# Softmax weights of two attention layers turned by SBUF transfers and 32x32 blocks on VectorE instead of on TensorE

## Chip, cores, metric

The kernel runs on one core of a Trainium2 chip. The metric is the device time in microseconds of one execution, taken as the median of several runs; a profile of one further execution gives the trace.

## What is computed

A stack of four graph layers works on 32 batch elements of 512 nodes with 256 channels, in float32, with one 512 x 512 adjacency for all. Each layer adds its result to its normalised input's residual:

```python
h = relu(layernorm(x)); x = x + layer(h, adj)
# layer 0: one head
e = leaky_relu((h @ W1) @ (h @ W2).T, 0.2), masked by adj
x += relu(softmax(e) @ (h @ W3))
# layers 1 and 3: four heads of 64, additive scores
e[i, j] = leaky_relu(dst[i] + src[j]), masked; x += elu(softmax(e) @ (h @ W))
# layer 2: four heads of 64, dot products
e = (Q K.T) / 8, masked
x += layernorm((softmax(e) @ V) @ Wo + bo) * gamma + beta
```

The softmax weights of layers 0 and 2 come out of the exponential with the query node on the partitions. The aggregation contracts over the other node, so they are needed with that one on the partitions: a transposition of a 512 x 512 matrix, once in layer 0 and four times (once a head) in layer 2, per batch element. Layers 1 and 3 form their weights turned from the start, since their scores are sums.

## The kernel before

A 512 x 512 matrix lies in SBUF as 128 partitions x 4 rows (t) x 512. The kernel is a software pipeline over the batch, with an order written out by hand for each engine. `slots` (L286) calls `first` for element 0, then `slot(a, b, c, d)` for n = 1 to 33 with a = element n, b = n - 1, c = n - 2, d = n - 3 (None outside 0 to 31). In one slot a goes through layer 0 and the beginning of layer 1, b through the rest of layer 1 and the beginning of layer 2, c through the rest of layer 2 and layer 3. Buffers are in three sets, s = element mod 3; the table BANK (L126) gives each product in PSUM one or two of eight banks. Semaphores alone bind the engines together, each engine runs its list strictly in order: `slot` for SP at L328, GpSimd L420, ScalarE L590, VectorE L841, TensorE L1158.

The work that the change and the steps of the prediction touch:
- `exp0` (L472) and `exp2` (L556), ScalarE, write one row t of the weights of layer 0 and of head h of layer 2, from what `masked_max0` (L662) and `masked_max2` (L781) on VectorE left.
- `weights_transposed0` (L1012) and `weights_transposed2` (L1110), TensorE: four 128 x 128 transposes of one row into a PSUM bank; `weights_out0` and `weights_out2` copy the bank to SBUF, half of them on ScalarE (L482, L565), half on VectorE (L692, L800).
- `aggregate0` (L1021) and `aggregate2` (L1129), TensorE, use the turned weights; the latter takes the heads in two pairs. `inverse_columns`, `inverse_spread` and `inverse_out` (L575 to L584, L1119) bring the inverse row sums into the layout of that product, `norm2` (L817) multiplies, `o_rows` (L1149) and `o_out` (L825) are the output product and its bias (L829 in the trace).
- `scores0`, `scores2`, `u_columns`, `v_rows`, `q_rows`, `qk_columns`, `transposed` (L958 to L1106) are the other products; `gat_weights` (L738) on VectorE and `gat_aggregate` (L1070) on TensorE are layers 1 and 3.
- `spread` (L316) on SP's queue writes the row factors of a layer of that kind to DRAM, waits, and reads them back broadcast to all partitions in two transfers; `gat_weights` waits for these. For two (element, layer) pairs, the first element's layer 1 and the last one's layer 3, TensorE broadcasts the first two heads itself (BY_PE, L218; L1066).
- `idle_turns` (L963) issues filler matmuls in the slots at either end.
- `load_next` and `store` (L312, L303), SP's queue, fetch x three elements ahead and write the result.

## Time and profile before

| | us |
|---|---|
| median of 3 runs | 2944.53 (2944.07 to 2944.73) |
| the profiled execution | 2943.7 |
| TensorE busy in it | 2887.3 (98%) |
| VectorE busy | 2127.5 (72%) |
| ScalarE busy | 1682.3 (57%) |
| GpSimd busy | 827.8 (28%) |
| HBM traffic | 105.5 MB, 36 GB/s over the span |

Busy time counts an engine's instructions, not its semaphore waits or the issuing of DMAs. Matmuls overlap each other, so TensorE's busy time is read as "never long without work" and the price of a matmul as the distance between two of them. The profiled span is 0.8 us below the median of the runs.

### The profile page before, as it was taken

What the parts mean: (1) busy time and instruction counts of PE and PEld (TensorE: products, weight loads), DVE (VectorE), ACT (ScalarE), POOL (GpSimd) and SP (SyncE); (2) the same over time, 40 slices, a digit from 0 to 9 for tenths busy, and PEclk for the clock granted to TensorE, in tenths of its full rate; (3) what the DMA queues carried; (4) which work ended last, traced back from release to release, by engine and by line L of the source; (5) the groups of instructions that cost most, each with busy time, mean ns of one, the idle gap of its engine ahead of it and who ended that gap; (6) DMA issues with size and microseconds to landing.
All of it is one profiled execution on the core that took longest, in us unless ns stands there. A gap on an engine that the chain in (4) does not pass through costs nothing.

```text
span 2943.7 us, 68275 instructions
## 1 busy us (share of the span) xinstructions
PE 2887.3 (98%) x27732; PEld 2034.8 (69%) x27732; DVE 2127.5 (72%) x5596; ACT 1682.3 (57%) x3554; POOL 827.8 (28%) x917
## 2 busy tenths in 40 slices
PE   7899999999999999999999999999999999999998
PEld 5566767666767666767667767667767667776766
DVE  5576787776787776877776877776877777877764
ACT  2555655655656655656655656656656656656543
POOL 2123222323222323222233232233222233222221
PEclk9999999999999999999999999999999999999999
DMA  3001011101011101011101011101011111011010
GB/s 102 22 23 45 27 41 45 44 23 45 23 44 45 44 23 44 23 44 44 38 30 44 23 45 44 37 30 44 23 45 44 34 33 40 28 37 37 17 36 30
DMA packets 58840, 109.89 MB, mean 37 GB/s; under 512 B 5568, under 2 KB 41408, under 8 KB 58528
## 3 DMA queue, kind: packets, MB, share of 16 engines
q1 hardware_dynamic: 58032, 104.61, 10.8%
q8 instruction: 220, 3.60, 0.5%
q0 software_dynamic: 496, 0.92, 0.3%
q14 instruction: 92, 0.75, 0.1%
HBM read 88.21 MB, written 17.30 MB: 36 GB/s over the span
## 4 chain that ended last, share of the span: by engine, by line
PE 77%; DVE 12%; POOL 6%; issue 2%; ACT 1%; SPq 0%; DMA 0%; POOLq 0%; DVEq 0%; ACTq 0%
PE ps L972 19%; PE ps L1080 11%; PE ps L1106 8%; PE ps L1115 8%; PE ps L978 8%; PE ps L1142 8%; PE ps L1029 8%; PE ps L958 4%; DVE stats L641 3%; POOL rstd L367 3%; POOL xc L417 3%; DVE pB L753 2%; PE ps L1017 2%; DVE nb L658 1%; DVE hn L829 1%
## 5 line engine op out<-in xcount | busy, mean ns | idle before, releaser
L389 POOL TENSOR_TENSOR qx<-qx,xc 128x512 f32<-128x512 f32 x128 | 163.7, 1279 | 869.4 <-ACT qx L529 869.4
L641 DVE BATCH_NORM_STATS2 stats<-xc 128x6 f32<-128x256 f32 x384 | 134.7, 413 | 328.6 <-POOL xc L399 264.1
L448 ACT ACTIVATE hn<-xc,nb,rstd 128x256 f32<-128x256 f32 x384 | 209.1, 592 | 163.9 <-DVE nb L658 160.7
L1080 PEld LDWEIGHTS ps<-vals,pA 128*64 128x64 f32 x8192 | 253.9, 138 | 54.6 <-issue 54.5
L972 PE MATMUL ps<-wgat,hT 128*128 128x264 f32 x1024 | 267.4, 395 | 1.8 <-ACT hT L457 1.8
L1080 PE MATMUL ps<-vals,pA 128*64 128x65 f32 x8192 | 266.4, 223 | 2.1 <-DVE pA L753 2.0
L1080 PE MATMUL ps<-vals,pB 128*64 128x65 f32 x8192 | 264.0, 223 | 0.3 <-DVE pB L753 0.2
L1080 PEld LDWEIGHTS ps<-vals,pB 128*64 128x64 f32 x8192 | 249.7, 138 | 16.8 <-issue 16.7
L457 ACT COPY hT<-ps 128x1024 f32<-128x1024 f32 x128 | 129.7, 1013 | 224.0 <-PE ps L958 219.8
L1106 PE MATMUL ps<-qx,qT 64*128 64x512 f32 x1024 | 249.8, 614 | 1.1 <-DVE hn L767 0.8
L364 POOL TENSOR_SCALAR rstd<-mv 128x4 f32<-128x4 f32 x160 | 75.0, 469 | 610.2 <-DVE mv L650 610.2
L1029 PE MATMUL ps<-vals,pB 128*128 128x256 f32 x1024 | 243.2, 381 | 1.1 <-ACT vals L469 1.1
L1142 PE MATMUL ps<-pX,vals 128*64 128x512 f32 x512 | 233.6, 599 | 2.3 <-DVE pA L806 2.3
L978 PE MATMUL ps<-hT,wqkvo 128*128 128x512 f32 x512 | 233.0, 598 | 0.8 <-ACT hT L457 0.8
L1008 PE MATMUL ps<-hT,qT 128*128 128x512 f32 x512 | 228.3, 599 | 1.1 <-ACT qT L463 1.1
L1029 PEld LDWEIGHTS ps<-vals,pB 128*128 128x128 f32 x1024 | 190.6, 191 | 38.9 <-issue 14.8
L972 PEld LDWEIGHTS ps<-wgat,hT 128*128 128x128 f32 x1024 | 179.5, 190 | 50.4 <-issue 24.9
L958 PE MATMUL ps<-ident,hn 128*128 128x128 f32 x1024 | 199.0, 280 | 11.9 <-ACT hn L448 11.1
L958 PEld LDWEIGHTS ps<-ident,hn 128*128 128x128 f32 x1024 | 132.3, 141 | 105.3 <-DVE rowmax L667 32.7
L367 POOL TENSOR_TENSOR rstd<-rstd,minus_half 128x4 f32<-128x4 f32 x160 | 192.5, 1203 | 13.3
L753 DVE SCALAR_TENSOR_TENSOR pA<-qT,gval,adjT 128x512 f32<-128x512 f32 x248 | 184.5, 785 | 6.7 <-DMA hT<-r_dram 6.5
L562 ACT ACTIVATE pX<-pX,negmax 128x512 f32<-128x512 f32 x256 | 183.4, 720 | 0.6 <-DVE negmax L797 0.6
(147 smaller groups left out, 6194.3 us busy)
## 6 DMA issues: line engine op xcount, KB each, us to landing
qT<-r_dram SPq DMA_DIRECT2D x64, 512.0 KB, 3.9
hT<-r_dram SPq DMA_DIRECT2D x64, 512.0 KB, 4.9
x_in<-in_x SPq DMA_DIRECT2D x32, 512.0 KB, 3.9
out_x<-xc SPq DMA_DIRECT2D x32, 512.0 KB, 3.0
...
r_dram<-growT SPq DMA_DIRECT2D x64, 8.0 KB, 1.3
...
```

The source lines that it names most:

```text
L367: nc.gpsimd.tensor_tensor(rstd[s][:, :], rstd[s][:, :], minus_half[:, :], ALU.pow).then_inc(rstd_ready[norm].sem, 1)
L641: last = nc.vector.bn_stats(stats[s][:, t, :], src[:, t, :])
L753: last = nc.vector.scalar_tensor_tensor(out=gat_p[s][h % 2][:, t, :], in0=row, scalar=gval[s][:, 1, t, h:h + 1], in1=adjT[:, t, :], op0=AL ...
L958: last = nc.tensor.transpose(ps[:, bank + k, t * P:(t + 1) * P], hn[s][:, t, k * P:(k + 1) * P], ident[:, :])
L972: last = nc.tensor.matmul(at, src[w.s][:, k, t * P:(t + 1) * P], wt[:, k, 0:width], start=(k == 0), stop=(k == KT - 1))
L978: last = nc.tensor.matmul(ps[:, bank + m, :], wt[:, k, m * P:(m + 1) * P], hT[w.s][:, k, :], start=(k == 0), stop=(k == KT - 1))
L1008: last = nc.tensor.matmul(ps[:, BANK[f"E{t}"], :], qT[s][:, k, t * P:(t + 1) * P], hT[s][:, k, :], start=(k == 0), stop=(k == KT - 1))
L1029: last = nc.tensor.matmul(rows_in(BANK["A"])[:, t, :], pB[s][:, t, j * P:(j + 1) * P], vals[s][:, j, 0:C], start=(j == 0), stop=(j == NT - 1))
L1080: last = nc.tensor.matmul(ps[lo:hi, BANK[f"G{g}.{h}"], t * DV:(t + 1) * DV], gat_p[s][h % 2][:, j, t * P + lo:t * P + hi], vals[s][:, j, h ...
L1106: last = nc.tensor.matmul(ps[:, BANK[f"S{p}.{t}"] + hh, :], qT[s][at, p, t * P:(t + 1) * P], kT[s][at, p, :], start=True, stop=True)
L1115: last = nc.tensor.transpose(ps[:, BANK[f"PT{h}.{t}"], j * P:(j + 1) * P], prob2[w.s][h][:, t, j * P:(j + 1) * P], ident[:, :])
L1142: last = nc.tensor.matmul(ps[hh * D:(hh + 1) * D, BANK[f"G2.{p}"], :], vals[s][:, j, h * D:(h + 1) * D], probT2[s][h][:, :, j * P:(j + 1) ...
```

## The change

The five transpositions per element no longer use TensorE and PSUM. SP's queue issues for each 512 x 512 tile of weights 16 SBUF to SBUF transfers: the tile is cut into 4 bands of 32 partitions, and a transfer takes from source band a the column blocks of 32 that belong to b, and writes them to band b of a scratch tile. VectorE then transposes all 32 x 32 blocks of one 128 x 512 row at a time from the scratch tile back over the weights (`turned0`, `turned2`). There are two scratch tiles; a third and later move waits until VectorE has emptied its tile. The moves come in a fixed order, layer 0 of a, then the four heads of b, each after all four exponentials of its tile.

The order lists of all engines are new, now over `slot(z, a, b, c, d, e)` with z = n + 1 for n = 1 to 34: layer 0's statistics of z are taken one slot early, the last half of layer 3's norms, its elu and its store belong to d. The PSUM table is new. x has two input buffers instead of three; some semaphores are shared. BY_PE is dropped (both pairs go through `spread`), and the filler matmuls in the ordinary slots are dropped, those of `first` stay.

```diff
+    X_SETS = 2
+    RING = 2
+    LAST = 3
...
-        x_in = sets("x_in", [P, NT, C])
+        x_in = [sb(f"x_in{s}", [P, NT, C]) for s in range(X_SETS)]
...
-        probT2 = [[pX[2], pA[s], pB[s], pX[2]] for s in range(SETS)]
+        probT2 = prob2
...
+        scratch = [pX[2], sb("scratch1", [P, NT, N])]
...
-        BY_PE = {(0, 1): (1, 3), (B - 1, 3): (1, 0)}
-        r_by_pe = sem("r_by_pe")
-
-        def lone(w, g):
-            return list(BY_PE).index((w.c, g)) if (w.c, g) in BY_PE else None
...
+        MOVES = (
+            (0, (0,)), (1, (2, 0)), (1, (2, 1)), (1, (2, 2)), (1, (2, 3)),
+        )
...
+            def emptied(self, eng, w, tile):
+                i = self.at[w.c, tile]
+                if i >= RING:
+                    c, old = self.steps[i - RING]
+                    (pT0_dve if old[0] == 0 else pT2_dve[old[1]]).wait(eng, Work(c), NT)
...
+        def bands(tile, band, column):
+
+            rows_of = tile[32 * band:32 * (band + 1), :, :].rearrange("p t n -> p (t n)")
+            return rows_of.rearrange("p (j b c) -> p j b c", b=P // 32, c=32)[:, :, column, :]
+
+        def move(sp, w, tile, weights):
+            slot = moves.slot_of(w, tile)
+            for a in range(P // 32):
+                for b in range(P // 32):
+                    sp.dma_start(bands(scratch[slot], b, a), bands(weights, a, b)).then_inc(moves.sems[slot], 16)
...
+            def move0(w):
+                if w is None:
+                    return
+                p0_ready.wait(sp, w, NT)
+                moves.emptied(sp, w, (0,))
+                move(sp, w, (0,), pA[w.s])
+
+            def move2(w, h):
+                if w is None:
+                    return
+                p2_ready[h].wait(sp, w, NT)
+                moves.emptied(sp, w, (2, h))
+                move(sp, w, (2, h), prob2[w.s][h])
+
+            def slot(z, a, b, c, d, e):
+                spread(b, 1); load_next(b); store(d); move0(a); spread(c, 3); move2(b, 0); move2(b, 1); move2(b, 2)
+                move2(b, 3)
...
-            def weights_out0(w, t):
-                if w is None:
-                    return
-                pT0p_ready.wait(act, w, t + 1)
-                nc.scalar.copy(pB[w.s][:, t, :], ps[:, BANK[f"PT{t}"], :]).then_inc(pT0_act.sem, 1)
...
+            def slot(z, a, b, c, d, e):
+                elu_relu(d, 3, 0); elu_min(d, 3, 0); elu_exp(d, 3, 0); elu_relu(d, 3, 1); elu_min(d, 3, 1)
+                elu_m[3].wait(act, d, 2); normalised(a, 0, 0); normalised(a, 0, 1); normalised(a, 0, 2)
+                normalised(a, 0, 3); elu_exp(d, 3, 1); h_transposed(a, 0); normalised(c, "in", 0)
+                normalised(c, "in", 1); normalised(c, "in", 2); normalised(c, "in", 3); u_out(a); elu_min(b, 1, 0)
+                elu_relu(b, 1, 0); elu_exp(b, 1, 0); elu_relu(b, 1, 1); elu_min(b, 1, 1); elu_exp(b, 1, 1)
+                v_out(a, 0); normalised(c, 3, 0); normalised(c, 3, 1); normalised(c, 3, 2); normalised(c, 3, 3)
+                h_transposed(c, 3); normalised(b, 2, 0); normalised(b, 2, 1); normalised(b, 2, 2); normalised(b, 2, 3)
+                h_transposed(b, 2); q_out(c, 3, 0); exp0(a, 0); exp0(a, 1); exp0(a, 2); exp0(a, 3); q_out(c, 3, 1)
+                biased_out(b, "KT", 0); biased_out(b, "QT", 0); biased_out(b, "QT", 1); gat_row_exp(c, 3)
+                biased_out(b, "KT", 1); gat_exp(c, 3); exp2(b, 0, 0); exp2(b, 0, 1); exp2(b, 0, 2); exp2(b, 0, 3)
+                exp2(b, 1, 0); exp2(b, 1, 1); exp2(b, 1, 2); relu0(a, 0); relu0(a, 1); relu0(a, 2); relu0(a, 3)
+                exp2(b, 1, 3); inverse_columns(b, 0); exp2(b, 2, 0); exp2(b, 2, 1); exp2(b, 2, 2); exp2(b, 2, 3)
+                exp2(b, 3, 0); normalised(a, 1, 0); normalised(a, 1, 1); normalised(a, 1, 2); normalised(a, 1, 3)
+                exp2(b, 3, 1); h_transposed(a, 1); inverse_out(b, 0); exp2(b, 3, 2); exp2(b, 3, 3); q_out(a, 1, 0)
+                inverse_columns(b, 1); q_out(a, 1, 1); gat_row_exp(a, 1); gat_exp(a, 1); inverse_out(b, 1)
+                v_out(b, 2)
...
+            def turned0(w, t):
+                if w is None:
+                    return
+                moves.landed(dve, w, (0,))
+                nc.vector.transpose(pA[w.s][:, t, :], scratch[moves.slot_of(w, (0,))][:, t, :]).then_inc(pT0_dve.sem, 1)
+
+            def turned2(w, h, t):
+                if w is None:
+                    return
+                moves.landed(dve, w, (2, h))
+                nc.vector.transpose(prob2[w.s][h][:, t, :],
+                                    scratch[moves.slot_of(w, (2, h))][:, t, :]).then_inc(pT2_dve[h].sem, 1)
+
+            def slot(z, a, b, c, d, e):
+                gat_norm(d, 3, 2); turned2(c, 2, 2); turned2(c, 2, 3); gat_norm(d, 3, 3); turned2(c, 3, 0)
+                turned2(c, 3, 1); turned2(c, 3, 2); turned2(c, 3, 3); norm2(c, 0); gat_out(d, 3, 0); gat_out(d, 3, 1)
+                gat_weights(b, 1, 0, 0, 1); norm2(c, 1); gat_weights(b, 1, 0, 2, 3); gat_weights(b, 1, 1, 0, 1, 2, 3)
+                o_out(c); statistics(c, "in"); mean_and_variance(c, "in"); gat_weights(b, 1, 2, 0, 1, 2, 3)
+                shift_of_norm(c, "in"); gat_weights(b, 1, 3, 0, 1, 2, 3); times_gamma(c); gat_norm(b, 1, 0)
+                gat_norm(b, 1, 1); gat_norm(b, 1, 2); gat_norm(b, 1, 3); statistics(c, 3); mean_and_variance(c, 3)
+                gat_out(b, 1, 0); mv_ready[3].wait(dve, c, 2); statistics(z, 0); gat_out(b, 1, 1); shift_of_norm(c, 3)
+                statistics(b, 2); mean_and_variance(b, 2); masked_max0(a, 0); masked_max0(a, 1); lrelu0(a, 0)
+                shift_of_norm(b, 2); lrelu0(a, 1); masked_max0(a, 2); mean_and_variance(z, 0); masked_max0(a, 3)
+                softmax_shift0(a); second_vectors(a); lrelu0(a, 2); lrelu0(a, 3); inverse_sum0(a); gat_max_t(c, 3); gat_max(c, 3)
+                gat_shift(c, 3); masked_max2(b, 0, 0, 0); masked_max2(b, 0, 0, 1); gat_rows_out(c, 3)
+                masked_max2(b, 0, 1, 0); masked_max2(b, 0, 1, 1); masked_max2(b, 0, 2, 0); masked_max2(b, 0, 2, 1)
+                turned0(a, 0); masked_max2(b, 0, 3, 0); masked_max2(b, 0, 3, 1); softmax_shift2(b, 0); turned0(a, 1)
+                masked_max2(b, 1, 0, 0); turned0(a, 2); masked_max2(b, 1, 0, 1); turned0(a, 3)
+                gat_weights(c, 3, 0, 0, 1, 2, 3); gat_weights(c, 3, 1, 0); masked_max2(b, 1, 1, 0)
+                masked_max2(b, 1, 1, 1); masked_max2(b, 1, 2, 0); masked_max2(b, 1, 2, 1); inverse_sums2(b, 0)
+                masked_max2(b, 1, 3, 0); masked_max2(b, 1, 3, 1); statistics(a, 1); softmax_shift2(b, 1)
+                mean_and_variance(a, 1); gat_weights(c, 3, 1, 1); turned2(b, 0, 0); turned2(b, 0, 1); turned2(b, 0, 2)
+                shift_of_norm(a, 1); turned2(b, 0, 3); gat_weights(c, 3, 1, 2, 3); gat_weights(c, 3, 2, 0, 1)
+                turned2(b, 1, 0); turned2(b, 1, 1); turned2(b, 1, 2); turned2(b, 1, 3); gat_norm(c, 3, 0)
+                gat_weights(c, 3, 2, 2); inverse_sums2(b, 1); gat_weights(c, 3, 2, 3); gat_weights(c, 3, 3, 0, 1)
+                shift_of_norm(z, 0); gat_max_t(a, 1); gat_weights(c, 3, 3, 2); gat_max(a, 1); turned2(b, 2, 0)
+                gat_weights(c, 3, 3, 3); gat_shift(a, 1); gat_norm(c, 3, 1); turned2(b, 2, 1); gat_rows_out(a, 1)
...
-            def weights_transposed2(w, h, t):
-                if w is None:
-                    return
-                p2_ready[h].wait(pe, w, t + 1)
-                for j in range(NT):
-                    last = nc.tensor.transpose(ps[:, BANK[f"PT{h}.{t}"], j * P:(j + 1) * P],
-                                               prob2[w.s][h][:, t, j * P:(j + 1) * P], ident[:, :])
-                last.then_inc(pT2p_ready[h].sem, 1)
...
+            def slot(z, a, b, c, d, e):
+                aggregate2(c, 0); pT2_dve[3].wait(pe, c, 4); aggregate2(c, 1); transposed(a, 0, 0)
+                transposed(a, 0, 1); transposed(a, 0, 2); transposed(a, 0, 3); o_rows(c, 0); o_rows(c, 1)
+                o_rows(c, 2); o_rows(c, 3); u_columns(a, 0); gat_aggregate(b, 1, 0); o_ready.wait(pe, c)
+                gat_aggregate(b, 1, 1); u_columns(a, 1); v_rows(a, 0, 0); gat_aggregate(b, 1, 2)
+                gat_aggregate(b, 1, 3); v_rows(a, 0, 1); gnorm[1].wait(pe, b, 3); scores0(a, 0); v_rows(a, 0, 2)
+                v_rows(a, 0, 3); scores0(a, 1); v0_ready.wait(pe, a); scores0(a, 2); transposed(c, 3, 0)
+                transposed(c, 3, 1); transposed(c, 3, 2); transposed(c, 3, 3); scores0(a, 3); masked0.wait(pe, a, 2)
+                q_rows(c, 3, 0); transposed(b, 2, 0); q_rows(c, 3, 1); transposed(b, 2, 1); transposed(b, 2, 2)
+                transposed(b, 2, 3); q_rows(c, 3, 2); q_rows(c, 3, 3); qk_columns(b, "QT", 0); masked0.wait(pe, a, 4)
+                qk_columns(b, "KT", 0); qk_columns(b, "KT", 1); qk_columns(b, "QT", 1); gat_max_across(c, 3)
+                gat_max_spread(c, 3); scores2(b, 0, 0); qT_ready.wait(pe, b, 2); scores2(b, 0, 1); gat_rows(c, 3)
+                kT_ready.wait(pe, b, 2); scores2(b, 0, 2); masked2[0].wait(pe, b, 2); scores2(b, 0, 3)
+                masked2[0].wait(pe, b, 4); scores2(b, 1, 0); scores2(b, 1, 1); pT0_dve.wait(pe, a); aggregate0(a, 0)
+                pT0_dve.wait(pe, a, 2); aggregate0(a, 1); pT0_dve.wait(pe, a, 3); aggregate0(a, 2)
+                pT0_dve.wait(pe, a, 4); aggregate0(a, 3); masked2[0].wait(pe, b, 8); scores2(b, 1, 2)
+                masked2[1].wait(pe, b, 2); scores2(b, 1, 3); agg0_norm.wait(pe, a, 4); gat_aggregate(c, 3, 0)
+                masked2[1].wait(pe, b, 6); v_rows(b, 2, 0); v_rows(b, 2, 1); v_rows(b, 2, 2); v_rows(b, 2, 3)
+                transposed(a, 1, 0); transposed(a, 1, 1); inverse_spread(b, 0); transposed(a, 1, 2)
+                transposed(a, 1, 3); gat_aggregate(c, 3, 1); q_rows(a, 1, 0); q_rows(a, 1, 1); gnorm[3].wait(pe, c)
+                q_rows(a, 1, 2); q_rows(a, 1, 3); gat_max_across(a, 1); inverse_spread(b, 1); gat_max_spread(a, 1)
+                gat_aggregate(c, 3, 2); gat_rows(a, 1); gat_aggregate(c, 3, 3)
```

## Rows read from the trace of the kernel before

**Rows 1.** The page's first part: span, busy time, share and instructions of each engine.
```profile
span 2943.7 us, 68275 instructions
...
PE 2887.3 (98%) x27732; PEld 2034.8 (69%) x27732; DVE 2127.5 (72%) x5596; ACT 1682.3 (57%) x3554; POOL 827.8 (28%) x917
```

**Rows 2.** One steady slot by windows: PE, PEld, DVE, ACT, POOL busy (instructions), PEclk, DMA.
```profile
1466.00:1554.40 88.40, 88.02 (x852) 61.71 (x849) 65.66 (x175) 52.22 (x110) 25.38 (x29) 1.00 0.12 37
```

**Rows 3.** Instructions of line 829, once a slot: durations, first and last start.
```profile
L829 DVE TENSOR_TENSOR hn<-ps,b_rows x32: 1223/1225/1226, 155.3 to 2894.6; 128x1024 f32<-128x1024 f32 x32
```

**Rows 4.** The chain in order of time, pieces of two slots: start, us, engine, line.
```profile
1429.57 1.72 PE ps L978 x4
...
1439.04 3.81 PE ps L1106 x16
...
1470.78 2.77 PE ps L1115 x24
...
1474.70 3.65 PE ps L1142 x16
1478.36 1.87 PE ps L1080 x64
...
1481.28 0.22 PE ps L958 x2
1481.50 0.87 PE ps L972 x4
```

**Rows 5.** VectorE's timeline in that slot: start, us, line, operation.
```profile
1474.37 2.70 DVE L753 SCALAR_TENSOR_TENSOR pA<-qT,gval,adjT 128x512 f32<-128x512 f32 x4
...
1553.05 0.67 DVE L806 COPY pX<-ps 128x512 f32<-128x512 f32 x1
1553.65 0.67 DVE L806 COPY pB<-ps 128x512 f32<-128x512 f32 x1
```

**Rows 6.** The page's costly groups, one of line 562: busy, mean ns.
```profile
L562 ACT ACTIVATE pX<-pX,negmax 128x512 f32<-128x512 f32 x256 | 183.4, 720 | 0.6 <-DVE negmax L797 0.6
```

**Rows 7.** The timeline of SP's queue in a steady slot: start, us of the issue.
```profile
1428.19 0.32 SPq L322 DMA_DIRECT2D r_dram<-growT  x1
1429.55 0.32 SPq L326 DMA_DIRECT2D qT<-r_dram  x1
1429.91 0.43 SPq L326 DMA_DIRECT2D hT<-r_dram  x1
1436.62 0.38 SPq L301 DMA_DIRECT2D x_in<-in_x  x1
```

**Rows 8.** The same queue in the first 20 us: start, us of all its issues.
```profile
3.33 1.92 SPq L338 DMA_DIRECT2D wgat<-in_L_gnn_W  x3
...
11.62 0.92 SPq L301 DMA_DIRECT2D x_in<-in_x  x2
```

**Rows 9.** The page's DMA issues: count, KB each, us to landing.
```profile
hT<-r_dram SPq DMA_DIRECT2D x64, 512.0 KB, 4.9
...
r_dram<-growT SPq DMA_DIRECT2D x64, 8.0 KB, 1.3
```

**Rows 10.** DMA from 1436 to 1445 us: packets by size, queue's share of 16 engines.
```profile
DMA packets 530, 0.55 MB, mean 61 GB/s; under 512 B 16, under 2 KB 528, under 8 KB 528
...
q1 hardware_dynamic: 528, 0.52, 17.6%
```

**Rows 11.** DMA from 9.4 to 10.8 us, the same two lines.
```profile
DMA packets 1014, 0.45 MB, mean 323 GB/s; under 512 B 764, under 2 KB 1004, under 8 KB 1014
...
q1 hardware_dynamic: 1014, 0.45, 118.1%
```

**Rows 12.** The chain near the end: lone rows, filler matmuls.
```profile
2919.93 0.45 PE ps L1066 x4
...
2926.10 2.05 PE ps L966 x16
```

**Rows 13.** Windows after a wait near the end; eighth column is the granted clock.
```profile
2840.50:2847.30 6.80, 6.03 (x8) 2.50 (x8) 0.28 (x1) 0.94 (x2) 2.49 (x5) 0.50 0.44 155
```

338 lines of the change are left out of this document (92 added, 246 removed), and 14 rows, old and new, of the table BANK.

## The prediction

> **What bounds the kernel now.** I read the page's first part first: TensorE is busy 98% of the span, VectorE 72%, ScalarE 57% [rows 1]. A busy share says little by itself, so next comes one steady slot (a slot is one pass over the written-out order, one batch element per pass): of 88.40 us TensorE is idle 0.38, VectorE works 65.66, ScalarE 52.22, and the DMA engines are busy 12% [rows 2]. The line that adds the output bias runs once per slot; its 32 starts lie from 155.3 to 2894.6, so the period is 2739.3 / 31 = 88.36 us, and 31 periods are all of the time but about 204 us at both ends [rows 3]. TensorE bounds it: in the chain its pieces follow one another without holes [rows 4].
>
> The chain's pieces give the price of each TensorE call, used below: 24 transposes 2.77 us (0.115 each), one pair of heads in aggregate2 3.65, one head of gat_aggregate 1.87, four matmuls of 256 columns 0.87, four of 512 columns 1.72, one scores2 call (four matmuls) 3.81 / 4 = 0.95 [rows 4].
>
> **The change, part by part.**
> *Removed from TensorE:* 16 transposes in layer 0 and 64 in layer 2, 80 x 0.115 = 9.2 us per slot. All lie on the path. The busy slot would go to 88.36 - 9.2 = 79.2 us.
>
> *VectorE:* before, 10 of the 20 rows of weights per slot were copied from PSUM here, a copy starting every 0.60 us [rows 5]; now 20 blockwise transposes. No row shows one. Nearest is that copy, same shape, 0.60; upper bound twice that, 1.20, if it passes the data twice; the lower bound is 0.30. I take 0.60: net +10 x 0.60 = 6.0 us, so VectorE works 71.7 of the slot, still below 79.2. *ScalarE* loses 10 copies and no longer matters by its sum. The 0.60 is weighed against a rule further down.
>
> *Added, on SP's queue:* five weight tiles per slot, each as 16 transfers (4 source bands x 4 destination bands) of 64 KB, in runs of 32 columns, which is 128 bytes: 512 runs per transfer, 32 per DMA engine. SP issued 8 transfers per slot (three for the row factors of each of layers 1 and 3, one load, one store; four of them in [rows 7]), now 88. The two prices of a transfer:
> - Issue: 0.38 us for a transfer of 512 runs (x_in), which with a gap of 0.05 is 0.43; two back to back took 0.92, 0.46 each [rows 8]; three in the crowded start took 1.92, 0.64 each [rows 8]. So 0.43 to 0.64; with the 0.36 between the starts of the two reads from r_dram as the lowest [rows 7].
> - DMA engine: in a stretch with nothing but 512 packets of 1 KB and 16 small ones the queue's share is 17.6% of 16 x 9 us, 25.3 us / 528 = 0.048 us a packet [rows 10]. In the start's stretch 764 packets are under 512 bytes (runs of 256 bytes, mostly) and 250 of about 1 KB: 118.1% of 16 x 1.4 us is 26.5 us; less 250 x 0.048 leaves 14.5 / 764 = 0.019 us each [rows 11]. A run of 128 bytes then costs between half of that, 0.0095, and all of it: 0.30 to 0.61 us for the 32 of one engine.
> Both ends include 0.43, the value of an unhurried issue. I take 0.44 us per transfer, a tile T = 16 x 0.44 = 7.0 us, range 5.8 (0.36) to 10.2 (0.64). The five tiles take 35 us of the slot, the other DMAs 12% of it [rows 2]: bandwidth is not short. Latency is what counts, since a transposition that took four matmul-like instructions now takes 7 us plus the landing, 1.3 us by the small store to r_dram [rows 9].
>
> A rule against this part: the 128-byte run. The rows show 0.019 us for runs of 256 bytes beside 0.048 for 1 KB, so small runs already cost more per byte. The Trainium skill (DMA: Bandwidth & Descriptors, Specifications) states that a transfer needs at least 512 bytes for line rate, below which the engine reads, modifies and writes; its section on why small descriptors are slow says SBUF to SBUF transfers don't suffer. By the first, 128-byte runs stay near the upper bound, T = 9.8 and a slower kernel; by the second they lie at the lower and the issue alone sets T.
>
> *The new waits, and what stands behind them.* move2 of a head starts only when all four exponentials of that head are done, and the four heads go one after another through SP, behind spread(c,3), with two scratch tiles. The aggregation of heads 2 and 3 waits for the last of them. That closes a loop from one slot's second aggregate2 to the next one's:
> 1. TensorE from the second aggregate2 to the fourth scores2 of heads 0 and 1, in the new order: 3.65; 24 transposes 2.7; 12 row calls (o_rows, v_rows, q_rows) x 0.87 = 10.4; 6 column calls x 1.72 = 10.3; scores0 4 x 1.72 = 6.9 (same shape); 4 gat_aggregate x 1.87 = 7.5; 4 scores2 3.8. Sum 45.3.
> 2. VectorE's two masked maxima, one turn and the shift 2.0, ScalarE's four exponentials 4 x 0.72 [rows 6] = 2.9, hops 0.4: 5.3.
> 3. Four tiles 4T, landing 1.3, four turns 2.5.
> 4. spread(b,1) is now queued behind move2 of the head before: issue 0.3, 1.3 to land, issues 0.36, then 4.9 [rows 7, 9] gives 6.9 after SP is free, while the aggregation is done 1.3 + 2.5 + 3.65 = 7.4 after it. gat_weights(b,1,0) stands ahead of norm2(c,1) on VectorE, 1.3 us of it; with a little crowding I put 2.0 us.
> Loop = 45.3 + 5.3 + 3.8 + 2.0 + 4T = 56.4 + 4T = **84.4 us** at T = 7.0. Above T = 7.2 move0 is late too (its turn stands ahead of the last masked maxima on VectorE, 9 us after the exponentials) and adds T - 7.2. The loop equals the old period at T = 7.8, 0.49 us per transfer. Below T = 5.7 the TensorE sum of 79.2 takes over.
>
> *The rest of the new order:* layer 0's statistics run a slot ahead, layer 3's last norms and output a slot later, so there is a 34th slot that holds only those; nothing is added to any engine, and the same chain ends the run. VectorE's idle 22.7 us of the slot [rows 2] covers it; if it doesn't, a late link costs its own length, 0.3 to 2 us, which the range has. *load_next and store* ride in SP's queue behind a move at worst; x_in has two buffers and is wanted a slot later: nothing, and 7 us of VectorE start if that cover is gone. The PSUM table gives freed banks to others; I cost it at nothing since TensorE's idle is 0.38 [rows 2], and its old waits could only return that much.
>
> *Both ends.* The two rows of weights that TensorE spread itself in the two lone cases (0.45 us [rows 12]) become the round trip through DRAM, 6.9 us, twice: +13. First tile of layer 0 exposed: T + 1.3 less adjacency work, +4. Fewer filler matmuls (16 in 2.05 us [rows 12]) leave the clock at 1.2 GHz more often, as after the wait at 2840.5, where the granted clock is 0.50 [rows 13]: +5. Shorter lone slot 32: -2. Sum +20.
>
> Total: 2943.7 - 31 x (88.36 - 84.4) + 20 = 2943.7 - 122.8 + 20 = 2841; the profiled execution lies 0.8 below the median of the runs (2944.53). I say **2845**.
>
> **The rivals.**
> - *TensorE keeps the bound* (moves hidden, T under 6): period 79.2 to 81 and nothing late: 2944 - 31 x 8.3 + 20 = 2707. For it: 0.36 us between two issues. Against: it needs a loop with no slack lost anywhere. Chance 0.20.
> - *The SP queue is the bound, slower.* Place: move2 of heads 0 to 3; price 4T; it decides from 0.49 us per transfer. At 0.56, T = 9.0, the loop is 56.4 + 36 + 1.8 = 94.2: 2944 + 31 x 5.8 + 20 = 3144; TensorE then stands still 10 us before each second aggregate2 and may get the 1.2 GHz clock after it [rows 13]. For it: 0.46 and 0.64 in back to back issues, and 0.019 us per packet. Against: steady issues are 0.38. Chance 0.31.
> - *VectorE becomes the bound*: a turn of 1.2 us makes its sum 65.7 - 6 + 24 = 83.7, and the loop grows by 5 turns, 3 us, with in-order waits on top: 87.5 to 90, 2944 + 20 + 20 = 2985. Chance 0.09. The Trainium skill (VectorE: DVE Perf Modes, The three transpose paths) has 311 ns for a 128x128 bf16 block transpose; if that scaled with the columns, 512 would take 1.24 us, this case.
> - *The forecast*, T 6.3 to 7.7: 2760 to 2925. Chance 0.40.
>
> **How the numbers follow.** A measurement of this kernel can tell 0.2% (6 us) from no change. Faster: 0.20 + nearly all of 0.40 less what the ends may eat = 0.56; within 0.2% 0.03; slower 0.41. The range takes in both neighbours: low 2705 (TensorE bound), high 3145 (T = 9). Left out are T near 10 (over 3300) and periods under 79. The likeliest case's own range is 2760 to 2925.
>
> **What would show it.** The bias line's 32 starts a period near 84.4 apart; SP's DMA issues near 0.4 us and 80 more per slot; turns of 0.60; TensorE idle 3 to 6 us before the second aggregate2, released by VectorE's turn, itself by the DMA. Wrong if that idle is absent (TensorE bound), or if issue-to-landing of the scratch transfers grows well beyond 2 us (engines or queue crowded).

## The result, and the profile of the changed kernel

The changed kernel takes **3587.12 us** (median of 4 runs, 3582.89 to 3588.69) against 2944.31 us (2944.07 to 2944.73) of the kernel before: ratio **1.218, 95% interval 1.216 to 1.220**, slower. The forecast was 2845 us, the range 2705 to 3145. The profiled execution took 3585.2 us.

Read in the order of the prediction, first the page's busy times, queue share and chain:

```profile
span 3585.2 us, 64705 instructions
...
PE 2838.3 (79%) x24860; PEld 1879.4 (52%) x24860; DVE 2299.7 (64%) x5916; ACT 1518.5 (42%) x3234; POOL 786.8 (22%) x917
...
q1 hardware_dynamic: 1409712, 272.55, 39.9%
...
SPq 46%; PE 33%; ACT 6%; issue 5%; DMA 5%; DVE 4%; POOL 0%; DVEq 0%; POOLq 0%; ACTq 0%
SPq L293 46%; PE ps L993 8%; PE ps L1084 7%; PE ps L1029 6%; PE ps L1134 5%; PE ps L999 3%; ACT pA L605 3%; PE ps L979 3%; ACT pA L528 2%; DVE pX L862 2%; DMA scratch<-pA 1%; DMA pX<-pA 1%; DMA scratch<-pX 1%; DMA pX<-pX 1%; DVE pA L806 1%
```

TensorE had 98% [rows 1] and has 79%. No engine is full. But 46% of the chain is one line of SyncE's queue, 293, the `dma_start` of `move`; in the kernel before SP's queue had 0% of the chain. DMA engines are busy 40% only: it is not the bytes that wait.

The bias line's 32 starts (it is line 840 now) against [rows 3], and one steady slot by windows, from one second aggregate2 to the next, against [rows 2]:

```profile
L840 DVE TENSOR_TENSOR hn<-ps,b_rows x32: 1216/1220/1225, 194.6 to 3529.2; 128x1024 f32<-128x1024 f32 x32
```

```profile
1800.50:1907.20 106.70, 85.54 (x774) 56.77 (x774) 70.97 (x185) 47.36 (x101) 24.16 (x28) 0.93 0.42 80
```

The period is (3529.2 - 194.6) / 31 = **107.57 us** against 88.36, which is 31 x 19.21 = 595.5 us of the 641.5 between the two profiled executions. The ends take 3585.2 - 3334.6 = 250.6 instead of 204.4, the other 46. VectorE works 70.97 us of the slot (third busy column; 71.7 was forecast), ScalarE 47.36.

The timeline of SP's queue in that slot shows where the time is; [rows 7] is its counterpart. "x16" is one tile, and the time that of all its issues:

```profile
1840.08 10.70 SPq L293 DMA_DIRECT2D scratch<-pA  x16
1850.83 0.61 SPq L356 DMA_DIRECT2D r_dram<-growT  x1
...
1857.67 11.55 SPq L293 DMA_DIRECT2D pX<-pA  x16
1869.32 10.70 SPq L293 DMA_DIRECT2D scratch<-pB  x16
1880.12 11.75 SPq L293 DMA_DIRECT2D pX<-pX  x16
1891.97 11.21 SPq L293 DMA_DIRECT2D scratch<-pX  x16
```

A tile takes 10.7 to 11.75 us where 7.0 was forecast, and the four heads follow one another without a gap: 1903.2 - 1857.67 = 45.5 us in which the queue does nothing but issue. The transfers of that line (duration of an issue in ns, least / median / most), and the page's time from issue to landing:

```profile
L293 SPq DMA_DIRECT2D pX<-pA x528: 585/630/1758, 34.4 to 3479.8; - x176
...
pX<-pA SPq DMA_DIRECT2D x528, 64.0 KB, 2.3
```

0.63 us and 0.04 to the next make 0.67 us per transfer, and 16 of them 10.7 us; a single long issue of 1.4 to 1.9 us in some tiles makes those 11.5 and more. What makes it long, no run shows. The landing is 2.3 us where 1.3 was taken from the small store [rows 9]. What waits at the end of it, in VectorE's and in TensorE's timeline (in brackets the idle time before, and its releaser):

```profile
1904.68 2.49 DVE L862 STREAM_TRANSPOSE pX<-scratch 128x512 f32<-128x512 f32 x4 [6.10 <-DMA scratch<-pX]
```

```profile
1800.50 5.22 PE L1134 MATMUL ps<-pX,vals 128*64 128x512 f32 x16 [5.78 <-DVE pX L862]
...
1907.22 3.68 PE L1134 MATMUL ps<-pX,vals 128*64 128x512 f32 x8 [6.21 <-DVE pX L862]
```

The four turns of the last head take 2.49 us, 0.62 each. TensorE stood idle 6.21 us before the second aggregation, released by the turn, the turn by the DMA: the waits that the prediction named as its sign. The aggregation behind such a wait takes 5.22 us where [rows 4] has 3.65; the next one's window has a granted clock of 0.50 (eighth column), which is 1.2 of 2.4 GHz, after those 6.2 us of idleness:

```profile
1907.20:1911.00 3.80, 3.78 (x10) 1.24 (x12) 2.36 (x4) 0.00 (x0) 0.00 (x0) 0.50 1.01 344
```

### The profile page after: what moved, and what is told of

The parts are those of the page before. It is cut to its first block, busy times and chain, and to the rows that moved or that the text cites. A ratio compares the mean times of both kernels' runs of the same rounds, so it can differ in the third digit from the quotient of the medians.

```text
span 3585.2 us, 64705 instructions
## 1 busy us (share of the span) xinstructions
PE 2838.3 (79%) x24860; PEld 1879.4 (52%) x24860; DVE 2299.7 (64%) x5916; ACT 1518.5 (42%) x3234; POOL 786.8 (22%) x917
## 3 DMA queue, kind: packets, MB, share of 16 engines
q1 hardware_dynamic: 1409712, 272.55, 39.9%
## 4 chain that ended last, share of the span: by engine, by line
SPq 46%; PE 33%; ACT 6%; issue 5%; DMA 5%; DVE 4%; POOL 0%; DVEq 0%; POOLq 0%; ACTq 0%
SPq L293 46%; PE ps L993 8%; PE ps L1084 7%; PE ps L1029 6%; PE ps L1134 5%; PE ps L999 3%; ACT pA L605 3%; PE ps L979 3%; ACT pA L528 2%; DVE pX L862 2%; DMA scratch<-pA 1%; DMA pX<-pA 1%; DMA scratch<-pX 1%; DMA pX<-pX 1%; DVE pA L806 1%
## 5 line engine op out<-in xcount | busy, mean ns | idle before, releaser
L426 POOL TENSOR_TENSOR vals<-qx,gval 128x256 f32<-128x256 f32 x256 | 153.6, 622 | 1281.4 <-ACT gval L563 1281.4
L993 PE MATMUL ps<-wgat,hT 128*128 128x264 f32 x1024 | 313.6, 454 | 132.2 <-DVE hn L786 128.9
L1040 PE MATMUL ps<-vals,pA 128*128 128x256 f32 x1024 | 258.6, 413 | 90.2 <-DVE pA L856 89.7
L1134 PE MATMUL ps<-pX,vals 128*64 128x512 f32 x512 | 183.6, 884 | 178.0 <-DVE pX L862 178.0
L993 PEld LDWEIGHTS ps<-wgat,hT 128*128 128x128 f32 x1024 | 216.5, 222 | 198.0 <-DVE hn L786 141.3
L1084 PE MATMUL ps<-vals,pB 128*64 128x65 f32 x8192 | 306.1, 242 | 11.1 <-DVE pB L772 11.1
L1084 PEld LDWEIGHTS ps<-vals,pB 128*64 128x64 f32 x8192 | 291.6, 156 | 25.7 <-issue 23.1
L1040 PEld LDWEIGHTS ps<-vals,pA 128*128 128x128 f32 x1024 | 207.3, 207 | 154.4 <-DVE pA L856 124.1
L1134 PEld LDWEIGHTS ps<-pX,vals 128*64 128x64 f32 x512 | 49.7, 204 | 311.0 <-DVE pX L862 206.4
L605 ACT ACTIVATE pA<-pA,negmax 128x512 f32<-128x512 f32 x128 | 90.8, 710 | 272.8 <-DVE negmax L816 272.8
```

The costliest lines, as they stand in the source:

```text
L605: nc.scalar.activation(row, row, ACT.Exp, bias=negmax[s][:, h, t:t + 1], scale=QK_SCALE, accum_out=rowsum[s][:, h, t:t + 1]).then_inc(p2_r ...
L993: last = nc.tensor.matmul(at, src[w.s][:, k, t * P:(t + 1) * P], wt[:, k, 0:width], start=(k == 0), stop=(k == KT - 1))
L1040: last = nc.tensor.matmul(rows_in(BANK["A"])[:, t, :], pA[s][:, t, j * P:(j + 1) * P], vals[s][:, j, 0:C], start=(j == 0), stop=(j == NT - 1))
L1084: last = nc.tensor.matmul(ps[lo:hi, BANK[f"G{g}.{h}"], t * DV:(t + 1) * DV], gat_p[s][h % 2][:, j, t * P + lo:t * P + hi], vals[s][:, j, h ...
L1134: last = nc.tensor.matmul(ps[hh * D:(hh + 1) * D, BANK[f"G2.{p}"], :], vals[s][:, j, h * D:(h + 1) * D], probT2[s][h][:, :, j * P:(j + 1) ...
```

## Experiments

Line numbers move with the edits: the bias line is 840 in the changed kernel, 841, 847, 848, 857 or 850 in the others. Times are medians of 2 to 4 executions; `shapes`, `half_runs`, `half_count`, `three_quarters` and `split_act` ran once each. The kernel before ran beside each at 2944.6 to 2945.5 us, and one profiled execution of each kernel gives its period.

### 1. What a transfer costs by itself

Theories A and C of the text below: the many short runs (A) or the DMA engines (C) set 0.67 us. Theory B: issuing has a fixed price for SBUF to SBUF. Behind the changed kernel's last store, with partitions, columns of a run, distance of the runs and their count:

```diff
+            SHAPES = [
+                (32, 32, 128, 16),
+                (32, 32, 128, 8),
+                (32, 32, 128, 4),
...
+                (32, 128, 512, 4),
...
+                (128, 32, 128, 16),
+                (64, 32, 128, 16),
...
+                (128, 256, 512, 4),
+            ]
...
+            for parts, size, step, count in SHAPES:
...
+                    sp.dma_start(runs(dst_t, lo, off, parts, size, step, count),
+                                 runs(src_t, lo, off, parts, size, step, count)).then_inc(tests, 16)
```

> The changed kernel, and behind its last store SP issues groups of 4 to 8 SBUF to SBUF transfers back to back, each group of another shape (partitions x runs x bytes of a run), waited for between groups; then ScalarE's queue and GpSimd's queue issue 8 of the move's own shape. In the changed kernel a move's transfer (32 partitions x 16 runs x 128 bytes) takes SP 0.63 us and a gap of 0.04, where a load of x (128 partitions x 4 runs x 1 KB, also 512 runs) took 0.38. Theory A, the issue grows with the runs that one DMA engine gets or with the runs per partition: 32 x 16 runs 0.63, 32 x 8 about 0.5, 32 x 4 about 0.4, and 128 partitions x 16 runs well over 1 us. Theory B, a fixed price of SBUF to SBUF or back to back transfers: all shapes 0.63. Theory C, the issue is held back by the DMA engines: then the time follows the bytes, shapes with runs of 64 bytes are cheaper than those of 128 and those of 512 bytes dearer. ScalarE's queue as SP's, 0.63; GpSimd's well over 1 us.

The numbers of a shape are partitions, floats in a run, floats from run to run, and runs per partition. Three stretches with 16, 8 and 4 runs of 128 B on 32 partitions, then the last shape, 128 partitions with 4 runs of 1 KB, beside the loads of x in the same execution, then ScalarE's and GpSimd's queues with the shape of `move`:

```profile
L422 SPq DMA_DIRECT2D scratch<-pX x8: 591/632/637, 3586.5 to 3591.2; - x8
...
L422 SPq DMA_DIRECT2D scratch<-pX x7: 610/611/612, 3593.9 to 3597.9; - x7
...
L422 SPq DMA_DIRECT2D scratch<-pX x6: 601/601/602, 3601.1 to 3604.3; - x6
...
L422 SPq DMA_DIRECT2D scratch<-pX x2: 607/624/642, 3667.1 to 3667.7; - x2
...
L336 SPq DMA_DIRECT2D x_in<-in_x x32: 368/432/438, 0.7 to 3201.3; - x32
...
L690 ACTq DMA_DIRECT2D scratch<-pX x8: 642/653/716, 3671.9 to 3676.7; - x8
...
L517 POOL DMA_DIRECT2D scratch<-pX x8: 649/649/764, 3679.2 to 3683.8; - x8
```

A quarter of the runs saves 0.03 of 0.63 us. Four runs of 512 B take 0.60 as four of 128 B do. The sharpest pair is the last shape: 0.61 and 0.64 us from SBUF where a load of x, of the same 128 partitions and runs but from DRAM, takes 0.43. Longer are only the transfers that move or cut up more: 512 runs of 256 B took 0.63 to 0.80 us, 1024 runs of 128 B 0.61 to 1.19, 2048 runs 0.59 to 2.58. Behind those of 2048 runs the engines are full: 7780 packets in 7 us at a share of 99.1%, 16 x 7 x 0.991 / 7780 = 0.014 us a packet. So what A or C describe shows only in transfers larger than those of `move`. For `move` itself: queue busy 39.9% of 16 x 3585.2, less before's 10.8% of 16 x 2943.7, over 1,351,680 packets more gives 0.0132 us, in the predicted 0.0095 to 0.019. A transfer has 528 packets, 33 per engine, so the engines would keep up with one each 0.43 us. **Theory B holds** for transfers of this size: about 0.6 us per SBUF to SBUF transfer, by whichever queue. The loads of [rows 7] that the price was taken from read or write DRAM; in the changed kernel's own slot they still take 0.33 to 0.43.

### 2. Half the runs, and half, ten and twelve of the transfers

```diff
-                    sp.dma_start(bands(scratch[slot], b, a), bands(weights, a, b))
+                    sp.dma_start(bands(scratch[slot], b, a)[:, 0:8, :], bands(weights, a, b)[:, 0:8, :])
...
-                for b in range(P // 32):
+                for b in range(2):
```

The first edit is half_runs. The second is half_count; three_quarters has range(3) there, and ten stops after the first ten pairs (a, b). All four leave blocks of the weights unturned, and GpSimd sets one scratch tile to zero once at the start.

> The changed kernel with all 16 transfers of every tile, each with 8 of its 16 runs per partition (the right half of the runs is left out, so half of the weights stay unturned): half the bytes and packets, the same number of issues. If an issue has a fixed price the total stays within 2% of 3585; if the issue's price grows with the runs (0.32 us as for the small store to r_dram plus 0.02 us for each run of a partition) a transfer takes about 0.48 with its gap 0.52, 80 x 0.15 = 12 us of the period go, total about 3190; if the DMA engines set the pace (0.43 us a transfer) the period halves its transfer part as with half the count, total about 2760.

> The changed kernel with 8 of the 16 transfers of every tile (destination bands 2 and 3 are left out, so half of the weights stay unturned). Theory of the loop through SP's queue: five tiles per slot lie on it, so 8 x 5 x 0.674 = 27 us of the period of 107.6 go, and at 80.6 the TensorE sum of 79.2 is nearly reached: period 80 to 83, total about 3585 - 31 x 26 - 20 = 2760 (2710 to 2840). Rival, that TensorE's 1.2 GHz stretches or late VectorE turns make a good part of the loss by themselves: period above 90, total above 3000.

> The changed kernel with 12 of the 16 transfers of each tile; the blocks of one band of rows are left out, so part of the weights is not turned. If the loop through SyncE's queue with its fixed price of 0.67 us per transfer sets the period, a tile takes 12/16 of 11.3 = 8.5 us and the slot 56.4 + 4 x 8.5 + 1.3 = 91.7 us; the ends lie between those of half_count (225) and of the changed kernel (251): 31 x 91.7 + 238 = 3081 us. If something other than the count of transfers gives the changed kernel its length (the turns, the new order of the work), the slot stays over 100 us and the time over 3300. If the stall that half_count still had (84.75 where the loop gave 78) belongs to every size, the slot comes to 96 to 98 us and the time to 3230.

> The changed kernel with the first 10 of the 16 transfers of each tile (the other blocks are left out, so part of the weights is not turned): 10 x 0.67 + 0.3 = 7.0 us a tile, the value that the prediction took for all 16. If the wrong price of a transfer is all that was wrong, the slot is the predicted 56.4 + 4 x 7.0 = 84.4 us and the time 31 x 84.4 + 230 (ends, between half_count's 225 and three_quarters' 233) = 2846 us, the forecast's 2845. If the waits that half_count and three_quarters had beyond the formula (5.7 us at 8 transfers, 2.8 at 12) are there at 10 too, the slot is 88 to 89.5 us and the time 2960 to 3005 us: then the change would not have paid even at the price that was predicted.

The bias line in the four, in the order of half_runs, half_count, ten, three_quarters:

```profile
L841 DVE TENSOR_TENSOR hn<-ps,b_rows x32: 1212/1216/1224, 193.0 to 3465.8; 128x1024 f32<-128x1024 f32 x32
```
```profile
L841 DVE TENSOR_TENSOR hn<-ps,b_rows x32: 1209/1214/1224, 166.4 to 2793.7; 128x1024 f32<-128x1024 f32 x32
```
```profile
L841 DVE TENSOR_TENSOR hn<-ps,b_rows x32: 1214/1219/1225, 171.1 to 2907.1; 128x1024 f32<-128x1024 f32 x32
```
```profile
L841 DVE TENSOR_TENSOR hn<-ps,b_rows x32: 1214/1216/1224, 177.4 to 3107.2; 128x1024 f32<-128x1024 f32 x32
```

| kernel | time us | period us | four heads' issues | predicted loop with them | difference |
|---|---|---|---|---|---|
| half_runs (16, half the bytes) | 3523.15 | 105.57 | 44.3 | 56.4 + 44.3 + 3.9 = 104.6 | 1.0 |
| changed kernel (16) | 3587.12 | 107.57 | 45.5 | 56.4 + 45.5 + 4.2 = 106.1 | 1.5 |
| three_quarters (12) | 3164.94 | 94.51 | 34.8 | 56.4 + 34.8 + 1.5 = 92.7 | 1.8 |
| ten | 2962.08 | 88.26 | 29.4 | 56.4 + 29.4 + 0.2 = 86.0 | 2.3 |
| half_count (8) | 2852.61 | 84.75 | 23.8 | 56.4 + 23.8 = 80.2 | 4.6 |

The fourth column is from the first issue of head 0 to the last of head 3 in one slot; the fifth adds T - 7.2 with a quarter of it as T. Halving the bytes gives 2 us a slot; halving the count gives 23. The loop's formula holds within 1.0 to 2.3 us from 10 to 16 transfers. At 8 it doesn't: there another bound has come. The slot of half_count by windows, TensorE's waits over that execution (us in total, times, longest), and one wait of TensorE and one of VectorE in that slot:

```profile
1522.40:1607.20 84.80, 79.67 (x775) 53.17 (x774) 70.49 (x185) 47.07 (x101) 24.16 (x28) 1.00 0.33 70
```
```profile
PE ps L980 <- ACT hn L498: 95.9, 36, 15.5
PE ps L1059 <- DVE dm L733: 29.8, 33, 0.9
PE ps L1065 <- DVE dmax L740: 22.2, 63, 0.5
```
```profile
1604.23 3.29 PE L994 MATMUL ps<-wqkvo,qT 128*128 128x256 f32 x14 [1.41 <-DVE qT L834]
```
```profile
1602.16 1.41 DVE L773 SCALAR_TENSOR_TENSOR pA<-qT,gval,adjT 128x512 f32<-128x512 f32 x2 [1.74 <-DMA hT<-r_dram]
```

TensorE waits 3.6 us in each slot, in small pieces that no transfer causes: 2 for layer 1's norm, 0.9 and 0.7 around the maximum of the additive scores. This slot has 1.4 more, for the product that stands on VectorE behind weights waiting for the row factors, as part 4 of the prediction's loop has it; three of the eight slots from 1098.2 to 1776.2 have such a wait, of 1.2 us in the mean. Over these eight TensorE works 80.6 us a slot and waits 4.1, so about 84.7 is what this order takes, not 79.2, and no wait for a move is in it. The run `ten` comes nearest to the kernel that was predicted (6.7 to 8.0 us a tile, 7.35 in the mean of that slot): 2962 us, ratio 1.005 (1.003 to 1.008), **still not faster than before**.

### 3. Two queues

Theory B leaves a way out if the queues issue side by side: six of 16 transfers from ScalarE's queue behind the fourth exponential.

```diff
+            for n in range(BLOCKS):
+                a, b = divmod(n, P // 32)
+                if (n >= BLOCKS - ON_ACT) == act:
+                    eng.dma_start(bands(scratch[slot], b, a), bands(weights, a, b)).then_inc(moves.sems[slot], 16)
```

> The changed kernel with 6 of the 16 transfers of every tile issued by ScalarE, right behind the tile's fourth exponential, 10 by SP; nothing is left out. Loop theory: SP needs 6.7 us a tile, ScalarE 4.0 and the next head's exponentials 2.9, so T is about 7 in place of 11, and the loop 56.4 + 4 x 7 = 84.4 and some for ScalarE's later work: period 86 to 92, total 2890 to 3100. Rival, that the DMA engines set the issue's pace whoever issues: 10 and 6 issues together take as long as 16, total stays above 3450.

3436.02 us, period (3378.2 - 186.1) / 31 = 102.97, far above what was expected. Its issues by queue, and the chain:

```profile
L296 SPq DMA_DIRECT2D pX<-pX x320: 585/644/1893, 150.2 to 3355.6; - x160
...
L296 ACTq DMA_DIRECT2D pX<-pX x192: 593/904/1897, 150.2 to 3352.0; - x192
```
```profile
PE 44%; ACTq 22%; ACT 18%; DVE 7%; issue 5%; DMA 3%; POOL 1%; SPq 0%; POOLq 0%; DVEq 0%
```

While both issue, one transfer takes ScalarE 0.90 us (0.65 alone), and SP's ten take 7.5 to 8.6 us, not 6.7. And ScalarE's exponentials now stand behind its own issues: ScalarE's queue has taken SP's place in the chain. The Trainium skill (Perfetto Trace Analysis, DMA Instruction — HWDGE) says that the descriptor generator is shared by the issuing sequencers and locked for one at a time. The lengthened issues fit that; the runs don't separate it from the engines, which in two such stretches (1787.3 to 1794.8 and 1711.8 to 1720.3) were 88% and 78% busy with the two queues' packets.

### 4. What transfers cost those who don't wait for them

```diff
+                if c is not None:
+                    copies(2)
                 spread(a, 1); store(c)
+                if c is not None:
+                    copies(5)
                 spread(b, 3)
```

> The kernel before, all its work as it is, with transfers on SyncE's queue that nobody waits for: 56 in each full slot (16 and 12 runs of 128 B on 32 partitions, SBUF to SBUF, eight at a time, each eight waited for by SyncE alone), in the two stretches in which the queue has nothing else. 56 x 28/32 = 49 of the changed kernel's 80 transfers a slot in bytes. If transfers cost only through those who wait for them, the time stays within 0.5% of 2944 us. If their traffic (SBUF's ports, the DMA engines, the other transfers that land later) slows the engines' own work, the period grows: by 1% or more, over 2975 us.

`copies(n)` issues n times eight SBUF to SBUF transfers into a spare buffer, 56 in a full slot. 2976.54 us, ratio 1.011 (1.009 to 1.013), which is over the 0.5% of the one theory and, by the time alone, what the other asked for. The rows decide, the last two from the end of SP's queue:

```profile
q1 hardware_dynamic: 889520, 207.49, 34.3%
...
L850 DVE TENSOR_TENSOR hn<-ps,b_rows x32: 1224/1225/1226, 155.2 to 2894.0; 128x1024 f32<-128x1024 f32 x32
```
```profile
2939.66 0.39 SPq L311 DMA_DIRECT2D out_x<-xc  x1
2940.09 32.79 SPq L340 DMA_DIRECT2D spare<-mask_pos  x40
```

The period is 2738.8 / 31 = 88.35, as before to 0.01 us, with the queue's share at 34.3% instead of 10.8%. The last store is issued at 2939.66, against 2940.26 in the kernel before. The 31 us are the last forty copies, issued behind that store and waited for at the end of the kernel; nothing else waits for them. So the traffic slowed no engine here, and the whole surplus is this tail.

### 5. The last heads back on TensorE

If the four heads in a row are the loop, taking heads 2 and 3 off the queue should free it. TensorE transposes them at the start of the next slot, through four free banks:

```diff
-            (0, (0,)), (1, (2, 0)), (1, (2, 1)), (1, (2, 2)), (1, (2, 3)),
+            (0, (0,)), (1, (2, 0)), (1, (2, 1)),
...
+                weights_transposed2(c, 2, 1); weights_transposed2(c, 2, 2); weights_transposed2(c, 2, 3)
+                aggregate2(c, 0); weights_transposed2(c, 3, 0); weights_transposed2(c, 3, 1)
...
```

> The changed kernel with the weights of layer 2's heads 2 and 3 transposed by TensorE again (32 transposes, 8 evictions by ScalarE and VectorE, in four PSUM banks at the start of the slot), and only layer 0's tile and heads 0 and 1 moved by SyncE's queue. It computes all. By the theory that the queue's 0.67 us per transfer sets the period, the last tiles no longer stand in the loop: SyncE needs 3 x 11.3 = 34 us of a slot, all of it beside other work, and TensorE is the bound with 79.2 + 2/5 of 9.2 = 82.9 us a slot and some small stalls: 84 to 88 us, in all 2800 to 2950 us, at about 86 us 2880 and so faster than the kernel before (2944). Rival 1: the new order of the work is itself worse than the old one and the slot stays at 90 us or more: over 3000 us. Rival 2: the turns on VectorE, ahead of other work in its order, set the period: 95 us or more, over 3150.

3546.96 us, period 106.14: 1.4 us a slot gained, where some 21 were expected. SP's queue now has nothing but five small transfers for 65 us of a slot, yet three moves are in the chain, because VectorE's order has the turns of head 1 ahead of layer 3's first norm:

```profile
1755.83 2.49 DVE L876 STREAM_TRANSPOSE pB<-pX 128x512 f32<-128x512 f32 x4 [6.35 <-DMA pX<-pB]
1758.25 0.14 DVE L792 RECIPROCAL rinv<-ps 128x4 f32<-128x4 f32 x1
1758.43 0.42 DVE L794 TENSOR_TENSOR hn<-ps,rinv 128x256 f32<-128x256 f32 x1
```

and TensorE's q_rows wait for that norm. My expectation had counted SP's time and forgotten what is queued behind the turn. Two more kernels put the turns late, the second with head 1 on TensorE too:

```diff
-                turned2(b, 1, 0); turned2(b, 1, 1); turned2(b, 1, 2); turned2(b, 1, 3); gat_norm(c, 3, 0)
+                gat_norm(c, 3, 0)
...
+                turned2(b, 0, 0); turned2(b, 0, 1); turned2(b, 0, 2); turned2(b, 0, 3)
```

> As two_heads (heads 2 and 3 transposed by TensorE), but VectorE's turns of heads 0 and 1 no longer stand ahead of the third GAT head's work in its order: head 0's are the last of the slot, head 1's the eighth of the next, and the aggregation of heads 2 and 3 comes ahead of that of heads 0 and 1. In two_heads the slot was 106.1 us with three moves in the chain of waits and 66 us of other work behind them. If the order was what kept the period there, the slot is now the loop 39.6 (second aggregation to the last weights of layer 0) + 12.5 (first move) + 5 (last row maxima and exponentials) + 12 + 11.5 + 2.3 (two more moves and a landing) + 2.5 (turns) + 3.7 (aggregation) = 89 us, between 86 and 93: 2880 to 3100 us in all, at 89 us 2975. If it was not the order but something that heads 2 and 3 on TensorE cost by themselves (its waits for evictions), the slot stays over 98 us and the time over 3250.

> As two_heads_late, with head 1 transposed by TensorE too: only layer 0's tile and head 0 are moved, 32 transfers a slot. It computes all. The loop loses a move: 89 - 11.5 = 78 us, and TensorE's work is 79.2 + 3/5 of 9.2 = 84.7 us a slot, so it is TensorE that bounds: 84.7 to 90 us a slot, at 87 us 31 x 87 + 205 = 2900 us in all, and faster than the kernel before if the theory (0.67 us per transfer, as long as the transfers stand in the loop) is the whole story. Rival: the new order of the work has other waits of its own of 5 us a slot or more; then the slot is over 90 us and the time over 3000 us, although no move stands in the loop.

Other than their texts say, both leave out the transposes of the first two row tiles of layer 0's input in every slot, four transposes or, at the prediction's 0.115, 0.5 us of TensorE. 3255.8 us, period 97.26, and 3281.35 us, period 97.98: the late turns gave 8.4 us besides, the further head nothing. In one_head's chain another wait stands in the place:

```profile
1707.51 0.63 SPq L294
...
1708.18 1.85 DMA r_dram<-growT
...
1710.43 4.85 DMA hT<-r_dram
...
1715.97 2.07 DVE pA L779 x3
```

Layer 3's row factors are queued behind layer 0's move, and VectorE's weights of layer 3 stand ahead of heads 2 and 3's maxima; and the aggregation of layer 0 waits 2.36 us for its own turn.

### 6. The new order with no, one and two moves

```diff
-            (0, (0,)), (1, (2, 0)), (1, (2, 1)), (1, (2, 2)), (1, (2, 3)),
...
+                weights_transposed0(a, 0); weights_transposed0(a, 1); pT0_act.wait(pe, a, 1); aggregate0(a, 0)
+                weights_transposed0(a, 2); pT0_dve.wait(pe, a, 1); aggregate0(a, 1); weights_transposed0(a, 3)
```

only_head0 keeps `(1, (2, 0))` in MOVES, only_heads01 that and `(1, (2, 1))`.

> The changed kernel's order of the work and its PSUM table with no tile moved: TensorE transposes all five again, the evictions go back into the weights' own buffers. It computes all. TensorE's work is that of the kernel before, 88.4 us a slot. If the new order is sound and the moves alone made the changed kernel slow, the slot is 88.4 to 94 us (16 transposes and evictions stand in a row at the start of the slot), in all 2930 to 3130 us, at 91 us 3025. If the order itself is what costs (one_head had 98.0 us with two moves), the slot is 98 us or more and the time over 3240.

> As order_only, with head 0's tile moved by SyncE and turned by VectorE as the last work of its slot. It computes all. TensorE has 88.4 - 1/5 of 9.2 = 86.6 us a slot. The move takes 10.7 + 2.3 us and the turns 2.5, which start some 25 us ahead of the aggregation that reads them: nothing waits for it. If a move costs nothing where it stands in no loop of waits, this is order_only less 1.8 us a slot or 57 us in all (2870 to 3075 us). If moves cost by themselves (by VectorE's turns or by the traffic), it is not faster than order_only.

> As only_head0, with head 1 moved too and its turns eighth in the next slot. TensorE has 84.7 us a slot. Head 1's move starts when head 0's is issued, so it lands 23 + 2.3 us after head 0's exponentials; in one_head the slot's second half from there to the aggregation was 28 us with TensorE waiting part of it. If only the loop counts, this one is level with only_head0 or up to 2 us a slot faster, 84.7 to 90 us; if the second move already comes into the loop, it is 2 to 6 us a slot slower than only_head0. A time under 2944 us in either of the two would beat the kernel before.

| kernel | time us | ratio, interval | period us |
|---|---|---|---|
| order_only | 3289.59 | 1.117 (1.115 to 1.119) | 98.53 |
| only_head0 | 3280.13 | 1.114 (1.112 to 1.116) | 98.29 |
| only_heads01 | 3227.52 | 1.096 (1.094 to 1.098) | 96.63 |

The slot of order_only by windows, its longest waits of TensorE in that slot, then the aggregation of heads 2 and 3 in it and in only_head0, and that stretch of only_head0 by windows:

```profile
1703.30:1801.80 98.50, 90.86 (x856) 63.17 (x854) 65.66 (x173) 52.98 (x111) 23.71 (x29) 0.98 0.09 32
```
```profile
1723.59 1.18 PE L1002 MATMUL ps<-ident,hn 128*128 128x128 f32 x4 [2.35 <-ACT hn L501]
...
1751.92 1.83 PE L1002 MATMUL ps<-ident,hn 128*128 128x128 f32 x8 [2.02 <-ACT hn L501]
1753.68 3.65 PE L1189 MATMUL ps<-pX,vals 128*64 128x512 f32 x16
```
```profile
1744.10 5.35 PE L1189 MATMUL ps<-pX,vals 128*64 128x512 f32 x16
...
1744.10:1749.40 5.30, 5.30 (x17) 1.46 (x16) 2.08 (x3) 1.11 (x2) 0.00 (x0) 0.68 0.30 99
```

The same work as before, with 98.5 us a slot: 7.6 idle and some 2.8 more busy. By the expectation's own bound (98 us or more) the order itself costs. The waits of half_count are among it; the rest I put down to where the 64 transposes stand, in a row, with little between them to hide the norm's latency, which no run separates. So this bounds the order's own price from above, about 10 us a slot, and experiment 2 gives 5.5 over the sum of 79.2 with the moves in. The two moves that nobody waits for took 0.2 and 1.7 us off the slot, where 1.8 was expected for each. The first did take its 16 transposes off TensorE, but behind the same wait of 2.02 us the next aggregation now runs 5.35 us instead of 3.65, at a granted clock of 0.68 instead of 1.00: the clock took back 1.7 of the 1.8. No version here comes below the kernel before except half_count, which leaves out half of the blocks.

## Why the prediction was wrong, point by point

- **The step that failed is the price of a transfer**: "I take 0.44 us per transfer, a tile T = 16 x 0.44 = 7.0 us, range 5.8 (0.36) to 10.2 (0.64)". It is 0.67, and with the few long issues T = 45.5 / 4 = 11.4 us, above the upper end. The stated range of the time went only to T = 9; the T of 10.2 would have given 56.4 + 40.8 + 3.0 = 100.2 us a slot and some 3330 us, still below the 3587. The rows were right and of the wrong kind: all issues in them were of transfers with DRAM at one side. The three 0.64 of the crowded start [rows 8] were the nearest to the truth by their number, but they too are loads from DRAM. The profiled execution lies 744 us above the sum of 2841; going from `ten`, whose T of 7.35 is near the predicted 7.0, to all 16 transfers costs 3585.2 - 2964.3 = 621 of them.
- **The remaining 123 us**: "Loop = 56.4 + 4T". It came within 1.0 to 2.3 us a slot in four runs, partly because two errors offset each other. In the slot from 1800.50: to the first head's move 57.2 against 50.6 + (11.4 - 7.2) = 54.8, about the half clock's 1.6 and the landing's 1.0; the four tiles 45.5; landing and turns 4.0 against 3.8; the 2.0 for the row factors behind the last head did not come up. In two slots of `ten`, from 1751.15 and 1840.02, the first part took 55.2 and 54.2 us against 50.8, so it was sized 3.4 to 4.4 short, and only the first has the slow clock (its aggregation takes 5.20 instead of 3.65). `ten`'s period of 88.26 is 3.86 over the forecast's 84.4: 1.6 by its T of 7.35, 2.3 by the first part less the 2.0. 31 x 3.86 is 120 us, and the ends of `ten` add the last 4.
- **"The TensorE sum of 79.2 takes over" below T = 5.7** was wrong in kind, and the second step that failed: the new order was put at nothing, since VectorE's idle covers it. In half_count TensorE works 80.6 us a slot and waits 4.1, half of that in short chains through the norms, so 84.7 takes over and not 79.2. The rival of 2707 us was never to be had, and the forecast's own gain of 4 us a slot hardly.
- **The rival that came true** is "the SP queue is the bound, slower", with its place, its price of 4T and its point (0.49 us per transfer). It was given 0.31 and a T of 9.0; with the measured tiles it gives 106. The period breaks even at `ten`'s 7.35 us a tile (88.26 against 88.36), not at 7.8.
- **VectorE** was right: 0.62 us from turn to turn (0.60 taken), 70.97 us a slot (71.7). The rival with 1.2 us a turn is out. The scaling of the 311 ns in the Trainium skill (VectorE: DVE Perf Modes, The three transpose paths) to an estimated 1.24 us is not what the trace shows for 128x512 floats.
- **Short runs** were priced rightly: 0.0132 us per packet of 128 B, and the DMA engines are not what the kernel waits for. Per byte short runs are dearer all the same: with the engines full a packet of 128 B took 0.014 us, one of 1 KB 0.048 (`shapes` from 3667.5, 77.4% of 16 x 3.5 us over 902 packets), so a byte costs 2.3 times as much. Of the two sections of the Trainium skill that the prediction weighed (DMA: Bandwidth & Descriptors, Specifications and Why small descriptors are slow) the trace bears out neither in full: SBUF to SBUF does pay per byte for short runs, but less than would make them the bound. The kernel got slow, as the first would have had it, by another cause.
- **The ends** grew by 46 us, not 20. order_only has 3286.8 - 3054.4 = 232.4 for both ends, so 28 come with the order (the 34th slot among it), and the other 18 of the changed kernel I put down to the moves in lone slots.
